# Splitting GpSimd's product of h into two halves, and weaving the two hand-overs between the feed-forward and the attention pipelines in another order

## The reference, cut to what matters

```
x = x + 0.5 * ffn(layernorm(x))      # first feed-forward
x = x + attention(layernorm(x))      # 16 heads of 8, causal softmax
x = x + 0.5 * ffn(layernorm(x))      # second feed-forward, same weights

ffn(x):   gate = q(x) @ q(Wgate).T;  up = q(x) @ q(Wup).T     # 128 -> 352
          h    = silu(gate) * up
          return q(h) @ q(Wdown).T                            # 352 -> 128
q(t):     per block of 16 along the last dimension: scale = max|t| / 6,
          t / scale rounded to the grid of FP4, times scale
```

## Time and profile before

| | |
|---|---|
| runs | 493.34, 494.47, 497.21 us, median 494.47 |
| profiled execution | 496.8 us, span 495.1 us |
| PE busy | 399.1 us, 81% of the span |
| DVE busy | 429.0 us, 87% |
| ACT busy | 316.0 us, 64% |
| POOL busy | 264.4 us, 53% |
| PE's granted clock, mean | 0.95 of full speed |

### The profile page before, as it was taken

How to read it: one execution, slowest core, us unless ns; L and a number is a source line. 1 busy time by engine, 2 the same in 40 slices (tenths; PEclk the granted TensorE clock), 3 DMA queues, 4 the chain that set the end, 5 groups by cost and what they waited for, 6 DMA issues and landing times.

```text
span 495.1 us, 12393 instructions
## 1 busy us (share of the span) xinstructions
PE 399.1 (81%) x3433; PEld 290.8 (59%) x3433; DVE 429.0 (87%) x1132; ACT 316.0 (64%) x856; POOL 264.4 (53%) x484
## 2 busy tenths in 40 slices
PE   0557877887788799998999999988896788877786
PEld 0334656655565577776776777666553466656665
DVE  3797999999978958988889889888868989999995
ACT  3557778867532657777777777766673366556643
POOL 6463665756651646776767777655570422333321
PEclk9978999988996899999999999999899699999999
DMA  7986000001445333454444545550000000000001
GB/s 224 234 140 101 1 1 0 1 1 46 138 140 142 99 95 103 136 146 123 130 141 137 142 142 142 144 143 4 4 1 1 1 13 22 21 21 21 21 12 42
DMA packets 38440, 39.30 MB, mean 79 GB/s; under 512 B 1789, under 2 KB 35453, under 8 KB 36093
## 3 DMA queue, kind: packets, MB, share of 16 engines
q1 hardware_dynamic: 38397, 38.79, 30.0%
HBM read 21.91 MB, written 10.49 MB: 65 GB/s over the span
## 4 chain that ended last, share of the span: by engine, by line
PE 38%; issue 23%; DVE 13%; ACT 11%; POOL 7%; DMA 6%; POOLq 1%; ACTq 1%; SPq 0%; DVEq 0%
PE bank L1308 6%; PE bank L1335 5%; DMA q_stack<-nmT 5%; PE bank L1168 5%; PE bank L1169 4%; PE bank L1277 3%; PE bank L1197 3%; ACT probs L799 3%; POOL hq_out L555 3%; PE bank L1254 2%; DVE nm L1059 2%; PE bank L1365 2%; PE bank L1339 2%; POOL xq_out L555 1%; PE bank L1155 1%
## 5 line engine op out<-in xcount | busy, mean ns | idle before, releaser
L799 ACT ACTIVATE probs<-bank 128x512 f32<-128x512 f32 x192 | 111.3, 605 | 49.3 <-PE bank L1308 48.1
L1059 DVE TENSOR_REDUCE nm<-bank 128x2 f32<-128x512 f32 (+1 forms) x192 | 126.0, 679 | 11.1 <-PE bank L1277 10.8
L626 POOL TENSOR_SCALAR_AFFINE_SELECT probs<-probs 128x256 f32<-128x256 f32 (+1 forms) x192 | 90.7, 489 | 71.9 <-ACT probs L799 70.4
L1308 PE MATMUL bank<-q_stack,k_stack 75*128 75x256 bf16 (+1 forms) x512 | 74.8, 250 | 9.5 <-ACT probs L799 5.8
L1277 PE MATMUL bank<-k_stack,q_stack 127*128 127x256 bf16 (+1 forms) x512 | 76.1, 252 | 3.4 <-DVE nm L1059 3.3
L555 POOL TENSOR_TENSOR xq_out<-xq_grid,xq_scale 128x256 f32<-128x256 bf16 x32 | 24.5, 765 | 88.9 <-DVE xq_grid L903 88.9
L1168 PE MATMUL bank<-wguT,f_xT 128*128 128x352 f32 x128 | 58.6, 544 | 6.6 <-ACT f_xT L720 4.6
L727 ACT ACTIVATE f_silu<-bank 128x352 f32<-128x352 f32 x64 | 29.7, 464 | 50.1 <-PE bank L1169 49.0
L1197 PE MATMUL bank<-wdT,f_hT 128*128 128x128 f32 (+1 forms) x384 | 55.9, 283 | 1.4 <-ACT f_hT L738 1.4
L1197 PEld LDWEIGHTS bank<-wdT,f_hT 128*128 128x128 f32 (+1 forms) x384 | 52.1, 200 | 6.6 <-issue 0.9
L1169 PE MATMUL bank<-wguT,f_xT 128*128 128x352 f32 x128 | 54.2, 509 | 0.0
(11 more groups left out here) (150 smaller groups left out, 885.7 us busy)
## 6 DMA issues: line engine op xcount, KB each, us to landing
q_stack<-q_parts SPq DMA_DIRECT2D x16, 576.0 KB
k_stack<-k_parts SPq DMA_DIRECT2D x16, 576.0 KB
q_parts<-qk_parts SPq DMA_DIRECT2D x16, 192.0 KB, 2.1
k_parts<-qk_parts SPq DMA_DIRECT2D x16, 192.0 KB, 2.4
v_stack<-zeros_bf SPq DMA_DIRECT2D x1, 2048.0 KB, 10.0
k_parts<-qk_parts SPq DMA_DIRECT2D x16, 128.0 KB, 2.3
out_dram<-x_all SPq DMA_DIRECT2D x15, 128.0 KB, 1.8
q_stack<-mask_q SPq DMA_DIRECT2D x1, 1664.0 KB
```

The source lines that it names most:

```text
L626: nc.gpsimd.affine_select(out=v, in_=v, compare_op=ALU.is_ge, fill=0.0, base=0, pattern=[[0, heads], [1, P]], channel_multiplier=-1).then_ ...
L799: nc.scalar.activation(probs[:, c, :], ps[:, :], ACT.Exp, scale=SCALE).then_inc(done, 1)
L1059: nc.vector.tensor_reduce(nm[:, j, h0:h0 + n], ps[:, :].rearrange("p (h k) -> p h k", h=n), AX_X, ALU.max, negate=True).then_inc(done, 1)
L1308: last = nc.tensor.matmul(ps[:, w * n:w * n + w], k_stack[0:SROWS, s, HG * g + h, k0:k0 + P], q_stack[0:SROWS, s, HG * g + h, q0:T], start ...
```

## The change

1. `hr` on POOL multiplies only the first half of h (columns 0 to 351, the rows of `hT0`). A new step `hs`, one turn later, multiplies the second half. It stands behind `hq` and ahead of `xr`, and waits until DVE has made the exponents of the next h (`QEXPS`), except for the last batches. `hT0` waits for the first half alone (new semaphore `h_half_ready`), `hT1` for the second. The last batch stays as it was.
2. `c2` is on ACT for all batches. `third` waits, for the first three batches, for the exponents of an h, and stands behind `c1` in `WARM`.
3. FFN to attention: FFN turn 18 has no scores in it, turns 19 and 20 run alone, turn 21 runs with attention turn 4 (all first scores); attention turns 5 to 7 are plain full turns. The four `bias` steps of attention turns 1 to 4 follow in a row ahead of turn 5. In `WARM`, `v` moves behind `f.dn1` and `lnS` behind `f.h1`.
4. Attention to FFN: the leftovers of batches 14 and 15 (`n1`, `yT`, `wo`, `wa`, `sS`, `sA`, `sE`) are spread over second-FFN turns 3, 4 and 5, where before turn 3 had all of them; `AV0` to `AV3` of batch 14 move back by some steps.

```
-    "",
+    "hs",
-FFN_ORDER = "hT0 xT hT1 xq lnV gu0 lnS gu1 dn0 hq xr h0 h1 hr lnN dn1".split()
+FFN_ORDER = "hT0 xT hT1 xq lnV gu0 lnS gu1 dn0 hq hs xr h0 h1 hr lnN dn1".split()
 WARM = """
-third f.hT0 f.xT lnN bias f.hT1 f.xq f.gu0 xT xTc f.lnV f.gu1 qk c1 f.hq f.h0 lnS f.h1 lnA split lnE f.xr f.lnS v f.dn0 f.hr f.lnN
-f.dn1 c2 stack
+f.hT0 f.xT lnN f.hT1 f.xq f.gu0 xT xTc f.lnV f.gu1 qk c1 third f.hq f.h0 f.h1 lnS lnA split lnE f.hs f.xr f.lnS f.dn0 f.hr f.lnN f.dn1 v c2 stack
 """
 FIRST_SCORES = """
-third f.hT0 f.xT lnN bias f.hT1 f.xq f.gu0 xT xTc f.gu1 qk c1 v f.dn0 f.hq f.h0 f.h1 split f.hr f.xr f.dn1 stack S0 S1 S2 c2 S3 lnS S4
-lnA S5 lnE S6 S7 S8 S9 S10 S11
+third f.hs f.hT0 f.xT lnN f.hT1 f.xq f.gu0 xT xTc f.gu1 qk c1 f.dn0 f.dn1 f.hq f.h0 f.h1 split f.hr f.xr v c2 stack
 """
-FIRST_PROBS ... FIRST_VALUES ... REST_VALUES ...
+FIRST_REST = "f.hs f.hT0 f.hT1 f.dn0 f.dn1 f.hq f.hr"
+REST_TRANSPOSES = "f.hs f.hT0 f.hT1 f.dn0 f.dn1"
+REST_SCORES = "S0 S1 S2 lnS S3 f.hT0 S4 lnA S5 f.hT1 S6 lnE S7 f.dn0 S8 f.dn1 S9 S10 S11"
-              (19, 5, FIRST_PROBS), (20, 6, FIRST_VALUES), (21, 6, REST_VALUES), (None, 7, FULL)]
+              (19, None, FIRST_REST), (20, None, REST_TRANSPOSES), (21, 4, REST_SCORES), (None, 1, "bias"), (None, 2, "bias"),
+              (None, 3, "bias"), (None, 4, "bias"), (None, 5, FULL), (None, 6, FULL), (None, 7, FULL)]
-LAST_OUTPUT = "f.xT f.gu0 oT0 f.gu1 f.hq f.xq f.xr n0 f.h0 oT1 n1"
-LAST_STATS = "f.h1 f.hr yT yTc f.lnN wo wa sS sA sE"
+SECOND_GATES = "f.xT f.xq f.gu0 oT0 f.gu1 f.hq n0 f.xr f.h0 f.h1 f.hr f.lnN"
+THIRD_GATES = "f.hs f.xT f.xq f.gu0 oT1 f.gu1 f.hq n1"
+THIRD_PRODUCTS = "f.xr f.h0 f.h1 f.hr f.lnN yT"
+FOURTH_GATES = "f.hs f.hT0 f.xT f.hT1 f.xq f.gu0 yTc f.gu1 wo f.dn0 f.hq wa"
+FOURTH_PRODUCTS = "f.xr f.h0 sS f.h1 sA sE f.hr f.lnN f.dn1"
...
+                        pool.wait_ge(hquant.step, QSTEPS * (b + base + 1))
+                        rescale_half(0, s, h_half_ready)
+                def h_rescale_rest(b, s, it):
+                    if halved(base, b):
+                        return
+                    if not (isinstance(b, int) and b >= NB - 2):
+                        pool.wait_ge(hquant.step, QSTEPS * (b + base + 1) + QEXPS)
+                    rescale_half(1, s, hquant.ready)
...
+                if first(b, WOVEN_THIRDS):
+                    pool.wait_ge(hquant.step, QSTEPS * (b + BEHIND_EXPS) + QEXPS)
...
-                            pe.wait_ge(hquant.ready, n + 1)
+                            pe.wait_ge((h_half_ready, hquant.ready)[j], n + 1)
```

More of the change, by code:

```diff
@@ L106 @@
-"""
-FIRST_PROBS = """
-nmS third lnN S0 f.hT0 S1 nm f.hT1 xT xTc S2 f.hq f.dn0 f.dn1 stack qk S3 ST0 c1 S4 f.hr ST1 S5 split ST2 S6 lnS ST3 S7 lnA
-c2 S8 lnE bias S9 v ST4 S10 S11
-"""
-FIRST_VALUES = "nmS ST5 S0 f.hT0 third  ST6 lnN S1 f.hT1 nm  ST7 S2 f.dn0 f.dn1 stack  ST8 S3 xT xTc"
-REST_VALUES = """
-f.hT0 bias  ST9 S4 f.hT1  ST10 S5 f.dn0 f.dn1 lnS  ST11 lnA S6 AV0 AV1  ST0 lnE S7 qk  ST1 oc0 c1 S8  ST2 split S9 AV2 AV3
-ST3 c2 oc1 S10 v  ST4 S11
-"""
+third f.hs f.hT0 f.xT lnN f.hT1 f.xq f.gu0 xT xTc f.gu1 qk c1 f.dn0 f.dn1 f.hq f.h0 f.h1 split f.hr f.xr v c2 stack
@@ L121 @@
 LAST_VALUES = """
-ST5  ST6 f.xT  ST7 oT0 n0  ST8  ST9 AV0  ST10 AV1 f.xr  ST11 f.gu0 oT1 n1 oc0 yT f.gu1 yTc AV2 AV3 f.h0 wo f.h1 wa oc1
+ST5  ST6 f.xT  ST7 oT0 n0  ST8  ST9 AV0  ST10  ST11 f.xr f.gu0 AV1 f.gu1 oT1 n1 oc0 yT yTc AV2 AV3 f.h0 wo f.h1 wa oc1
 """
-LAST_OUTPUT = "f.xT f.gu0 oT0 f.gu1 f.hq f.xq f.xr n0 f.h0 oT1 n1"
-LAST_STATS = "f.h1 f.hr yT yTc f.lnN wo wa sS sA sE"
-SECOND_TURN = " ".join(f"f.{step}" for step in FFN2_ORDER)
+SECOND_GATES = "f.xT f.xq f.gu0 oT0 f.gu1 f.hq n0 f.xr f.h0 f.h1 f.hr f.lnN"
@@ L129 @@
-              (3, 22, LAST_STATS), (4, None, SECOND_TURN), (5, None, SECOND_TURN)]
+              (1, 20, LAST_PROBS), (2, 20, LAST_RESIDUAL), (2, 21, LAST_VALUES), (3, 22, SECOND_GATES),
+              (4, 22, THIRD_GATES), (None, 21, "sS sA sE"), (4, 22, THIRD_PRODUCTS), (5, 22, FOURTH_GATES), (5, 22, FOURTH_PRODUCTS)]
 VECTOR_COPIES = {"oc0": (14, 15), "oc1": (14,), "yTc": (13, 14), "f.xT": (0,)}
-POOL_PARTS = 5
+WOVEN_THIRDS = 3
+BEHIND_EXPS = 12
 TAIL = [(14, c) for c in range(5, CHUNKS)] + [(15, c) for c in range(CHUNKS)]
@@ L418, in macaron_kernel @@
         wT_filled, wT_read = sem("wT_filled"), sem("wT_read")
+        h_half_ready = sem("h_half_ready")
         f_sum_ready, f_squares_ready, f_var_ready = sem("f_sum_ready"), sem("f_squares_ready"), sem("f_var_ready")
@@ L564, in rescale_half @@
                     hquant.grid[:, s, I * j:I * j + I].rearrange("p (n k) -> p n k", k=BLOCK),
-                    hquant.scale[:, s, n * j:n * j + n].unsqueeze(2).to_broadcast([P, n, BLOCK]), ALU.mult).then_inc(last_ready, 1)
+                    hquant.scale[:, s, n * j:n * j + n].unsqueeze(2).to_broadcast([P, n, BLOCK]), ALU.mult).then_inc(ready, 1)
             def ffn(base, ps):
@@ L594, in h_rescale @@
                         for j in range(NT):
-                            rescale_half(j, s)
-                    else:
-                        rescale(hquant, b + base, s)
-                steps = {"xr": x_rescale, "hr": h_rescale}
+                            pool.wait_ge(last_step, HALF_STEPS * (j + 1))
+                            rescale_half(j, s, last_ready)
+                    else:
+                        pool.wait_ge(hquant.step, QSTEPS * (b + base + 1))
[6 more added lines that the diff above has]
+                    rescale_half(1, s, hquant.ready)
+                steps = {"xr": x_rescale, "hr": h_rescale, "hs": h_rescale_rest}
                 if not base:
@@ L605, in third_parts @@
                 pool.wait_ge(parts2_ready, b + 1)
+                if first(b, WOVEN_THIRDS):
+                    pool.wait_ge(hquant.step, QSTEPS * (b + BEHIND_EXPS) + QEXPS)
                 nc.gpsimd.tensor_tensor(qk_parts[:, s % PART_TURNS, 2, :], qk_rest[:, :], qk_parts[:, s % PART_TURNS, 1, :],
                                         ALU.subtract).then_inc(parts3_ready, 1)
-            def second_parts(b, s, it):
-                if first(b, POOL_PARTS):
-                    pool.wait_ge(taken["qk"], b + 1)
-                    nc.gpsimd.tensor_copy(qk_parts[:, s % PART_TURNS, 1, :], qk_rest[:, :]).then_inc(parts2_ready, 1)
             def bias(b, s, it):
@@ L655, in _ @@
             pool.wait_ge(bias_loaded, 16 * NT)
-            pool_steps = {"lnE": lambda b, s, it: inverse_std(aln, b), "sE": lambda b, s, it: inverse_std(gln, b), "third": third_parts, "bias": bias, "c2": second_parts}
+            pool_steps = {"lnE": lambda b, s, it: inverse_std(aln, b), "sE": lambda b, s, it: inverse_std(gln, b), "third": third_parts, "bias": bias}
             pool_steps.update({f"ST{c}": mask(c) for c in range(CHUNKS)})
@@ L769, in second_parts @@
             def second_parts(b, s, it):
-                if first(b, POOL_PARTS):
-                    return
                 act.wait_ge(taken["qk"], b + 1)
```

8 lines of the change are left out of this document (3 added, 5 removed).

## The result

The changed kernel is slower: 499.23 us, median of 20 runs (493.42 to 503.5), against 496.83 us (491.45 to 501.52) for 20 runs of the kernel before on the same chip. The ratio is 1.0065, with a 95% interval of 1.0038 to 1.0091: a small loss, but clear of the noise. I had forecast 487.5 us, with a range of 479 to 498, and 0.59 for faster. The prediction was wrong in its direction: it had a gain of 7 us where there is none, and the loss, at 0.65%, is smaller than the 1% that it wanted for a change that can be told.

The account below looks back on a forecast made before the run. The prediction took the FFN turn to be bound by the chain through the x product, second silu and magics to hq_sum; its terms, 0 + 0.3 + 0 - 5.4 - 1.5 - 0.4, gave -7.0 us, so 487.5 us, range 479 to 498.

Parts of the forecast that it names:

- Halves in the second FFN's loop: Second FFN's eleven turns: DVE's chain comes 0.59 us earlier, but hq_sum still waits for hq_magic; 0 us.
- the chain: FFN turn: x grid, POOL's x product, transpose, gate and up, second silu, both magics, hq_sum; as long as the 6.75 us turn.
- The first rival: FFN turns: DVE is the bound, so 0.59 us comes back in about 25 turns; 473 us, chance 0.10.
- Halves in the first FFN: First FFN's loop: the x sum waits for the second half, 0 to 0.15 us in each of six turns; +0.3 us.
- Woven turns: FFN turns 14 to 18: fewer DVE stalls against an x product 0.75 us later each turn; 0, between -2 and +3 us.
- The rest of the FFN and attention turns 4 to 7: Hand-over from FFN to attention: 55.3 us becomes 49.1 to 50.6, 4.7 to 6.2 us saved, -5.4 taken.
- the four biases lie under the row maxima: Ahead of attention turn 5: four biases of 0.73 us run beside row maxima, which don't use the port.
- the third rival: FFN-to-attention hand-over: it gives nothing, as attention turns 5 and 6 are slow for their own waits; about 493 us, chance 0.20.
- To the second FFN: Attention to second FFN, turns 3 to 6: spreading leftovers frees DVE and little else; -1.5 us, bounds -4 and +1.
- The slower rival: First FFN and woven turns: second half comes late to the port and blocks the x product; 499 us, chance 0.14.

Follow-up runs that it names:

- The x magic experiment: Changed kernel with ACT making the magic of x ahead of the second silu in both FFN loops: 497.68 us, ratio 0.9981 to the kernel before.

## Why the prediction was wrong, point by point

**Halves in the second FFN's loop, 0: right.** 74.25 for 74.28 us. DVE's idle gap came where I put it, on hq_magic and on the silu ahead of it, 2.6 and 2.1 us over the eleven turns by the waits of DVE in this stretch, so 0.43 a turn for my 0.6. xq_scale takes 0.16 to 0.21 us, the 0.2 that I gave as the sign. The x magic experiment confirms the chain. The first rival is out: 6.74 and 6.82 us a turn, not 6.2.

**Halves in the first FFN, +0.3: right**, 40.82 for 40.77 us. The half does hold up the x sum there, 0.65 us long for 0.28, and it costs nothing:

```profile
87.56 0.79 POOL L558 TENSOR_TENSOR hq_out<-hq_grid,hq_scale 128x352 f32<-128x352 bf16 x1
87.85 0.65 DVE L900 TENSOR_TENSOR xq_sum<-xq_odd,xq_magic 128x256 bf16<-128x256 bf16 x1
88.42 0.51 DVE L900 TENSOR_TENSOR hq_sum<-hq_odd,hq_magic 128x704 bf16<-128x704 bf16 x1
```

**Woven turns, 0 (between -2 and +3): mechanism right, sum wrong.** The step that failed is "I take 0": I set the half ahead of the x product against the stalls of DVE that the new order saves, and called it even. The 0.75 us for the half measured 0.7 and 0.75, the turn at full clock 8.98 for my 9.0. But the new orders alone, with the product whole, take 44.1 us, where the four profiles with the orders and the product of before take 46.7 to 48.6: they save 2.6 to 4.5 us, more than my bound of 2. The halves then give it all back and more. The six profiles with the half in front of the x product have 45.6 to 51.6 us, a mean of 49.7, against 44.3 in the four with the two exchanged: 5.4 us, and the medians of the timed totals differ by 4.9. Of that the half itself is about 2.5 (four turns of 0.62, 8.98 and 8.89 for 8.36 and 8.26 at full clock), the low clock the rest. This term alone takes the kernel from a ratio of 0.9963, which isn't told from 1, to 1.0065.

**The rest of the FFN and attention turns 4 to 7, -5.4: wrong, the step that failed was "the four biases lie under the row maxima".** They did so only in part, since `lnE` stood ahead of them in POOL's queue and waited 5.36 us, and they began 2.1 us before the split for their 2.8 us; I counted their length and port and not what they were queued behind. I had priced the loss of this cover at 2 to 3 us; it measured 3.4 (54.11 to 50.71) in the one profile that isolates it, with the clock of turn 5 in it, and 0.7 and 2.0 where the x product stands first (54.09 to 53.40 and 52.10), since turns 5 and 6 then ran partly at the low clock. The other part is the first scores, which I took at 8.3 to 9.8 us and which took 10.71, because TensorE had two batches' transposes and down products ahead of them; 1.3 of it came back. Here the last h made up for it, with 4.85 us where I had 5.7. With both undone the stretch is 50.8 us, or 50.3 from the end of the grid, where my 49.1 to 50.6 begin; the biases alone give as much (50.71). Turns 6 and 7 were right (12.62 and 12.48 for 12.2 and 12.5), and with them the third rival is out, that the hand-over gives nothing: its sign was a turn 6 over 16 us.

**Attention turns 8 to 15, not in the sum.** The profile had +4.1 us. With the wait behind the stores the two kernels agree to 0.01 us, one profile each, so the difference lives in the cycle of transfers. Whether a part belongs to the change isn't settled: the four profiles with the orders of before and the old transfers have 153.1 to 156.4 us, a mean of 154.7, and the nine with the new orders 153.8 to 160.6, a mean of 156.6.

**To the second FFN, -1.5: the number was met (-2.0) in part by luck.** The kernel before ran a part of this stretch at the low clock. In two profiles with the old order the beginning of it is at full clock, and the stretch takes 50.97 and 51.23 us; the new order takes 50.3 to 50.9 where it fares best, in seven of twelve profiles, so where the clock favours both it gains less than 1 us. And four of the twelve profiles with the new order, but none of the five with the old, took 53.5 to 56.3 us there, at a low clock. The means are 52.3 and 51.9: on average this term gave nothing. I had named a loss only as a bound of +1.

**The slower rival**, at 0.14 and 499 us, had the result and half the mechanism. The half does delay the x product, but by its place in POOL's queue and not by coming late to the port. It did so only in the woven turns, and their low clock was about half of its price.

**The base.** I worked from a median of 494.47; with 496.83 my forecast would have been 489.8, and no better in its direction.
